# A fused two-layer transformer kernel: expert input rows split into bf16 halves before they are turned, and turned by a DMA transposition instead of TensorE

## The reference

```python
xf = x.reshape(-1, dim)                              # 8192 rows of 256
scores = softmax(xf @ w_router.T)
expert_weights, expert_indices = top_k(scores, 2)    # two of eight experts for each row
h = silu(einsum('td,edh->eth', xf, w1)) * einsum('td,edh->eth', xf, w3)   # hidden width 352
y = einsum('eth,ehd->etd', h, w2)
out = sum(expert_weights[:, :, None] * y[chosen experts], axis=1)
```

## Time and profile before

| | |
|---|---|
| times of three runs | 1982.25, 1982.32, 1988.02 us (median 1982.32) |
| span of the profiled execution, first to last instruction | 1987.6 us (it has no other time of its own; of the three runs, 1988.02 is the nearest) |
| first attention, up to about | 572 us |
| experts: count and tables, first load, then 71 tiles | 572 to 1050 us |
| second attention | 1050 to 1560 us |
| ternary feed-forward | 1560 to 1987 us |
| TensorE busy | 1746.9 us, 88% of the span |
| DVE, ACT, POOL busy | 1466.4, 1418.6, 1006.9 us |
| expert rounds | 6.3 to 6.4 us each |

### The profile page before, as it was taken

How to read it: one execution, slowest core, us unless ns; L and a number is a source line. 1 busy time by engine, 2 the same in 40 slices (tenths; PEclk the granted TensorE clock), 3 DMA queues, 4 the chain that set the end, 5 groups by cost and what they waited for, 6 DMA issues and landing times. The chain is left out here.

```text
span 1987.6 us, 52512 instructions
## 1 busy us (share of the span) xinstructions
PE 1746.9 (88%) x16125; PEld 1469.8 (74%) x16125; DVE 1466.4 (74%) x4269; ACT 1418.6 (71%) x2753; POOL 1006.9 (51%) x1295
## 2 busy tenths in 40 slices
PE   4889999999729999999993999999999578888887
PEld 3667878787519998999992788888888366666666
DVE  4889999999434343333332999999998599999996
ACT  5888999999424443444442777777777499999998
POOL 3557888887523233322226676676662133333332
PEclk8899999999859999999996999999999799999999
DMA  5434343433234352222224455545552112212111
GB/s 173 155 111 146 117 128 110 132 109 95 81 97 143 93 83 85 89 84 89 89 78 92 102 125 113 122 110 121 116 119 68 54 49 64 63 63 63 63 58 54
DMA packets 190557, 194.16 MB, mean 98 GB/s; under 512 B 33184, under 2 KB 180128, under 8 KB 189408
## 3 DMA queue, kind: packets, MB, share of 16 engines
q1 hardware_dynamic: 165856, 157.88, 26.7%
q0 software_dynamic: 24576, 34.62, 8.5%
HBM read 118.13 MB, written 74.30 MB: 97 GB/s over the span
## 5 line engine op out<-in xcount | busy, mean ns | idle before, releaser
L1898 POOL TENSOR_TENSOR e_h_lo<-e_h 128x256 bf16<-128x256 f32 (+1 forms) x213 | 138.7, 652 | 334.3 <-DVE e_h L2012 334.3
L2012 DVE TENSOR_TENSOR e_h<-e_s,e_ps_ab 128x256 f32<-128x256 f32 (+1 forms) x213 | 89.3, 420 | 275.2 <-ACT e_s L1921 275.2
L2073 PE MATMUL e_ps_ab<-e_xt_hi,k_w_hi 128*128 128x256 bf16 (+1 forms) x852 | 233.3, 274 | 0.0
L2073 PE MATMUL e_ps_ab<-e_xt_hi,k_w_lo 128*128 128x256 bf16 (+1 forms) x852 | 233.0, 273 | 0.0
L2073 PE MATMUL e_ps_ab<-e_xt_lo,k_w_hi 128*128 128x256 bf16 (+1 forms) x852 | 233.0, 273 | 0.0
L1921 ACT ACTIVATE e_s<-e_ps_ab 128x256 f32<-128x256 f32 (+1 forms) x213 | 81.5, 383 | 148.3 <-PE e_ps_ab L2073 148.2
L2473 PE MATMUL f_ps_h<-f_qh,p_arena 128*128 128x256 bf16 x512 | 123.8, 281 | 35.1 <-DVE f_ql L2437 28.5
L1928 ACT ACTIVATE e_yo<-e_ps_y,e_xe 128x256 f32<-128x256 f32 x142 | 59.6, 471 | 112.7 <-PE e_ps_y L2073 112.7
L2473 PE MATMUL f_ps_h<-f_ql,p_arena 128*128 128x256 bf16 x512 | 122.9, 279 | 0.0
L2073 PE MATMUL e_ps_y<-e_w_hi,e_h 128*128 (+1 forms) x426 | 116.5, 273 | 0.0
L2073 PE MATMUL e_ps_y<-e_w_hi,e_h_lo 128*128 (+1 forms) x426 | 115.9, 272 | 0.0
(11 more groups left out here) (433 smaller groups left out, 6621.5 us busy)
## 6 DMA issues: line engine op xcount, KB each, us to landing
e_xe<-sent_rows SPq DMA_DIRECT2D x71, 272.0 KB, 2.8
back_rows<-e_yo SPq DMA_DIRECT2D x71, 256.0 KB, 2.1
x_rows<-a_x SPq DMA_DIRECT2D x64, 256.0 KB, 2.7
p_arena<-in_xT SPq DMA_DIRECT2D x32, 256.0 KB, 4.7
a_xa<-in_x SPq DMA_DIRECT2D x32, 256.0 KB, 4.8
a_xr<-in_x SPq DMA_DIRECT2D x32, 256.0 KB, 4.6
a_xa<-x_rows SPq DMA_DIRECT2D x32, 256.0 KB, 3.3
x_rows<-a_xa SPq DMA_DIRECT2D x32, 256.0 KB, 2.2
```

What stands on the lines that cost most here:

```text
L1898: nc.gpsimd.tensor_tensor(h_lo[0:k, b.par, c, :], h[0:k, b.par, c, :], h_hi[0:k, b.par, c, :], ALU.subtract).then_inc(mg.sem, 1)
L2012: nc.vector.tensor_tensor(h[0:k, b.par, c, :], s[0:k, c, :], ps_ab[0:k, c, N:2 * N], ALU.mult).then_inc(mh.sem, 1)
L2073: last = nc.tensor.matmul(to, left, right, start=(i == 0), stop=(i == len(terms) - 1))
```

## The change

The rows of a tile are now split into halves as they lie, before they are turned: ACT reads `xe` in SBUF, in two activations of 128x256, and writes bf16 into a new buffer `rows` (two tiles deep); DVE subtracts in two instructions likewise. SP then issues one DMA transposition per tile (`turn`), from `rows` in SBUF to `turned` in SBUF: 128 partitions by 8 blocks of 128 bf16 numbers, 256 KB, three tiles deep. TensorE no longer turns anything and reads `turned`. The loads are six tiles deep instead of four. A new semaphore `t_ld` tells that a tile is turned; `up` waits for it, and so does `rows_high`, since the transposition of two tiles ago must have read `rows` before it is written again. The splitting runs further ahead: in round b, ACT and DVE split tile b+3 (before: b+1). SP stores b, turns b+3, loads b+6.

```diff
+    XE, XT = 6, 3
-        xe = sb("xe", [P, 4, NT, WIDE], F32)
-        xt_hi, xt_lo = sb("xt_hi", [P, 2, KC, N], BF16), sb("xt_lo", [P, 2, KC, N], BF16)
+        xe = sb("xe", [P, XE, NT, WIDE], F32)
+        rows_ = sb("rows", [P, 2, 2, KC, NT, P], BF16)
+        turned = sb("turned", [P, XT, 2, KC, N], BF16)
-        ps_t = psum("ps_t", [P, 2, 512])
+        t_ld = [sem(f"e_t_ld{i}") for i in range(XT)]
+        def turned_away(eng, b):
+            if b is not None:
+                eng.wait_ge(t_ld[b.n % XT], 16 * (b.n // XT + 1))
...
+            def turn(b):
+                uv.wait(sp, b, "lo")
+                me.wait(sp, b.back(XT), "up2")
+                nc.sync.dma_start_transpose(turned[:, b.n % XT, :, :, :].rearrange("p h k (t n) -> p (h k t) n", t=NT),
+                                            rows_[:, b.par, :, :, :, :].rearrange("p h k t n -> p (h k t n)")).then_inc(t_ld[b.n % XT], 16)
-            for b in tiles[0:4]:
+            for b in tiles[0:XE]:
                 load(b)
+            for b in tiles[0:XT]:
+                turn(b)
...
             for b in tiles:
                 store(b)
-                if b.n + 4 < TILES:
-                    load(tiles[b.n + 4])
+                if b.n + XT < TILES:
+                    turn(tiles[b.n + XT])
+                if b.n + XE < TILES:
+                    load(tiles[b.n + XE])
...
             def rows_high(b):
-                ue.wait(act, b, "xT")
-                me.wait(act, b.back(2), "up2")
-                nc.scalar.activation(xt_hi[:, b.par, :, :].rearrange("p k n -> p (k n)"), ps_t[:, b.par, :], ACT.Copy).then_inc(ua.sem, 1)
+                act.wait_ge(e_ld[b.n % XE], 16 * (b.n // XE + 1))
+                turned_away(act, b.back(2))
+                for t in range(NT):
+                    last = nc.scalar.activation(rows_[:, b.par, 0, :, t, :], xe[:, b.n % XE, t, 0:D].rearrange("p (k n) -> p k n", k=KC), ACT.Copy)
+                last.then_inc(ua.sem, 1)
...
                     silu(b, c, k)
-                    if c == 0 and 0 < b.n < TILES - 1:
-                        rows_high(tiles[b.n + 1])
+                    if c == 0 and b.n + 3 < TILES:
+                        rows_high(tiles[b.n + 3])
...
             def rows_low(b):
                 ua.wait(dve, b, "hi")
-                me.wait(dve, b.back(2), "up2")
-                nc.vector.tensor_tensor(xt_lo[:, b.par, :, :].rearrange("p k n -> p (k n)"), ps_t[:, b.par, :],
-                                        xt_hi[:, b.par, :, :].rearrange("p k n -> p (k n)"), ALU.subtract).then_inc(uv.sem, 1)
+                for t in range(NT):
+                    last = nc.vector.tensor_tensor(rows_[:, b.par, 1, :, t, :], xe[:, b.n % XE, t, 0:D].rearrange("p (k n) -> p k n", k=KC),
+                                                   rows_[:, b.par, 0, :, t, :], ALU.subtract)
+                last.then_inc(uv.sem, 1)
...
             def up(b, c, at, k, e):
-                ua.wait(pe, b, "hi")
-                uv.wait(pe, b, "lo")
+                turned_away(pe, b)
                 mh.wait(pe, b.back(1), f"h{c}")
...
                     up(b, c, at, k, e)
-                    if c == 0 and 0 < b.n < TILES - 1:
-                        turn_tile(tiles[b.n + 1])
```

More of the change, by code:

```diff
@@ L1772, in experts @@
         I32 = mybir.dt.int32
-        ident, bases, ends, tri, iota, starts, ones, seen = sh.ident, sh.bases, sh.ends, sh.tri, sh.iota, sh.starts, sh.ones, sh.seen
+        bases, ends, tri, iota, starts, ones, seen = sh.bases, sh.ends, sh.tri, sh.iota, sh.starts, sh.ones, sh.seen
         zeros, w1, w3 = sh.zeros, sh.w1, sh.w3
@@ L1823, in experts @@
         s_count = sem("e_count")
-        e_ld = [sem(f"e_e_ld{i}") for i in range(4)]
+        e_ld = [sem(f"e_e_ld{i}") for i in range(XE)]
+        t_ld = [sem(f"e_t_ld{i}") for i in range(XT)]
         o_st = [sem(f"e_o_st{i}") for i in range(2)]
@@ L1829, in experts @@
         uv = Signal(sem("e_uv"), "lo")
-        ue = Signal(sem("e_ue"), "xT")
         me = Signal(sem("e_me"), "up0 up1 up2")
@@ L1861, in load @@
                 at = sp.value_load(row[0:1, b.n:b.n + 1], min_val=0, max_val=E * ROOM + SPARE - ROWS)
-                if b.n >= 4:
-                    my.wait(sp, b.back(4), "y1")
-                sp.dma_start(xe[:, b.n % 4, :, :], block_of(at)).then_inc(e_ld[b.n % 4], 16)
+                if b.n >= XE:
+                    my.wait(sp, b.back(XE), "y1")
+                sp.dma_start(xe[:, b.n % XE, :, :], block_of(at)).then_inc(e_ld[b.n % XE], 16)
+            def turn(b):
[3 more added lines that the diff above has]
+                                            rows_[:, b.par, :, :, :, :].rearrange("p h k t n -> p (h k t n)")).then_inc(t_ld[b.n % XT], 16)
             def store(b):
@@ L1928, in results @@
                     nc.scalar.activation(yo[:, b.par, t, :], ps_y[:, b.par, t * D:(t + 1) * D], ACT.Copy,
-                                         scale=xe[:, b.n % 4, t, D:D + 1]).then_inc(my.sem, 1)
-            rows_high(tiles[0])
-            rows_high(tiles[1])
+                                         scale=xe[:, b.n % XE, t, D:D + 1]).then_inc(my.sem, 1)
+            for b in tiles[0:3]:
+                rows_high(b)
             for b in tiles:
@@ L2053, in prepare @@
                     nc.vector.tensor_scalar(pre.half_tg[:, :], pre.tg[:, 2:3], 0.5, None, ALU.mult).then_inc(wv, 1)
-            rows_low(tiles[0])
-            rows_low(tiles[1])
+            for b in tiles[0:3]:
+                rows_low(b)
             for b in tiles:
@@ L2059, in _ @@
                     hidden(b, c, k)
-                    if c == 0 and 0 < b.n < TILES - 1:
-                        rows_low(tiles[b.n + 1])
+                    if c == 0 and b.n + 3 < TILES:
+                        rows_low(tiles[b.n + 3])
                 if b.n == 4:
@@ L2074, in product @@
                 return last
[L2076 to L2081, removed]
             nc.tensor.matmul(ps_y[:, 1, 0:E], ones[:, :], seen[:, :], start=True, stop=True).then_inc(s_count, 1)
@@ L2099, in up @@
                     last = product(ps_ab[0:k, c, i * N:(i + 1) * N],
-                                   [(w[:, kc, bass.ds(e, 1), at:at + k].rearrange("p o k -> p (o k)"), x[:, b.par, kc, :])
-                                    for kc in range(KC) for w, x in ((hi, xt_hi), (hi, xt_lo), (lo, xt_hi))])
+                                   [(w[:, kc, bass.ds(e, 1), at:at + k].rearrange("p o k -> p (o k)"), turned[:, b.n % XT, part, kc, :])
+                                    for kc in range(KC) for w, part in ((hi, 0), (hi, 1), (lo, 0))])
                 last.then_inc(me.sem, 1)
@@ L2112, in down @@
                 last.then_inc(md.sem, 1)
-            turn_tile(tiles[0])
-            turn_tile(tiles[1])
             before = None
```

## The result

The changed kernel takes 1989.7 us (median of 20 runs, 1981.72 to 1997.95), the one before 1984.1 us on the same chip (20 runs, 1982.23 to 1988.3). The ratio is 1.0025, 95% interval 1.0016 to 1.0033: a quarter of a per cent slower, 5 to 6 us, where 2100 us was forecast, 117.5 us slower. Its profiled execution has a span of 1990.1 us, against 1987.6. So the direction was right by a hair and the size was wrong by a factor of twenty.

What follows compares the result with a forecast made beforehand. TensorE was taken to bound the expert stage before, the closed loop after, at 3.1 + 4.9 = 8.0 us a round: +112 us on 68 rounds, +5.5 for the start, so 1982.3 + 117.5 = 2100 us, range 1954 to 2350.

Steps and rivals of the forecast that it cites:

- a loop from `y1`: Expert stage: ACT's split waits for a transposition issued behind `y1`, closing one lap per round of 3.1 us plus transposition time.
- +112 us: Expert stage rounds: 8.0 us a round, 1.65 more than now, on 68 rounds.
- X: Time of one DMA transposition from issue to landing, taken as 4.9 us, ends 2.8 and 13.3 kept for the range.
- turning point: Transposition time of 3.25 us, issue to landing: under it the round gains, beyond it the round loses.
- no change: Balance case: transposition time in a narrow band from 3.1 to 3.3 us leaves the time unchanged; chance 0.06.
- 3.1 for the rest of the lap: Per round without the transposition: `y1` to store's issue 0.39, split 0.85, silu 0.76, `results` 0.84, hand-overs 0.24 us.
- the 30 us: TensorE in the expert stage: gain over 68 rounds from rounds of 5.9 us instead of 6.35.
- my rival of the copy's pace: Transposition lands in 2.8 us, the loop takes 5.9, just TensorE's round; time 1956 us, chance 0.22.
- 5 us for `places`: Queue of the early loads: once, the 13.3 us transfer `places` can delay a transposition, some 5 us left in the range.
- The removed transpositions: TensorE, between pieces 0 and 1 of a round: four transpositions cost 0.44 us.
- The longer start: Start of the expert stage: six loads instead of four go ahead of the first transposition; first product 5.5 us later.
- the rival in which the clock stays low: TensorE, busy 74%, falls to 1.2 GHz, its 54 products taking 11.5 us a round; time 2338 us, chance 0.10.

Runs made afterwards that it cites:

- experiment 1: Changed kernel with the transposition of tile b+3 issued ahead of the store of tile b: 1975.91 us, ratio 0.9894 to the kernel before.
- experiment 3: Changed kernel without the third product of each pair of halves, 42 matrix products a round instead of 54: ratio 0.9983 to the kernel before.
- experiment 4: Changed kernel with 42 matrix products a round instead of 54 and the transposition issued ahead of the store: 1894.6 us, ratio 0.9492 to the kernel before.
- experiment 9: Changed kernel with `rows` three tiles deep instead of two, loads still six deep, transposition behind the store: ratio 0.9919 to the kernel before.
- experiment 10: Changed kernel with each transposition issued as two, high halves and low halves, behind the store: ratio 1.0225 to the kernel before.
- experiment 11: Changed kernel with each transposition issued as two, high and low halves, ahead of the store: ratio 0.9868 to the kernel before.
- experiment 6: Changed kernel with `rows` three tiles deep instead of two and loads five deep instead of six: ratio 1.0569 to the kernel before.

## Why the prediction was wrong

**The mechanism was right.** The prediction put the bound in a loop from `y1` over the store's issue, the transposition, the split, silu and results, and experiments 1, 3, 4, 9, 10 and 11 all confirm it. That loop is why nothing was gained. The forecast of +112 us rested on two sizes in it. That the three turned tiles don't help, since the two-deep `rows` closes the loop, holds too: experiment 9 changes that depth alone and wins 1.0%.

**The step that failed is the size of X.** I took 4.9 us, scaling the price of a piece in `places` by 1024 pieces of 256 bytes. The trace after shows that there are 1024 such packets per tile, but each takes 18 ns at the median, some 21 on average in a quiet round, and the whole lands in 3.2 us; the price of a 16-byte piece written to memory does not carry over to these 256-byte pieces written to SBUF. The other row, `slot_i`, had given 2.9, and the nearest plain row, the load of 272 KB, 2.8. The sum's largest term, +112 us, hung on that choice, between two rows that disagreed by 2 us a round around a turning point at 3.25. I saw the turning point and still gave no change 0.06; it is what came, with a median X inside the band of 3.1 to 3.3.

**A second term was mis-sized, 3.1 for the rest of the lap.** It measures 2.5 to 2.6. I had added durations; activations in a row overlap, so two splits take 0.72 and not 0.85, two silus 0.63 and not 0.76, and the hand-overs are largely in that. With X = 3.2 and 2.6, the quiet lap is 5.8 and the gain would have been the 30 us less the start, as in my rival of the copy's pace. My 3.1 with the right median X gives a round of 6.3, so no change: right by luck, since the 0.5 us too much stands where the spread of X should.

**Why that gain did not come.** The mean of X up to the start of the split is 3.84 us, not its median of 3.26, and 2.6 + 3.84 = 6.44, against a measured mean round of 6.42. A loop 0.15 us under TensorE's 5.90 can absorb next to nothing of a long X, so the average is what counts. That X varies was left out, but for 5 us for `places`, which cost 10.2 us over two rounds here and 3.4 before. Why X varies is open in part: the packets of instructions coincide with the long ones, and no run took them away.

**The smaller terms.** The removed transpositions are worth 0.44 us a round: right, rounds of 5.90 where nothing else binds. The longer start: 5.5 us forecast; first load to first product went from 5.6 to 10.2 us, so 4.6. The splits on ACT and DVE are 0.41 and 0.42 us a piece, and hidden, apart from the lap. The clock stayed at 1.00 but for the 10.2 us behind `places`. There 26 products went at 0.21 us apart instead of 0.11 (752.45 to 757.96), so the fall cost some 2.6 us of the 10.2, an estimate; the rival in which the clock stays low is not what happened. (Its sum has a slip: 54 products at 0.21 are 11.3 us, not 11.5, and its time 2328.)

The Trainium skill's rule that transposing DMAs are as fast as ordinary ones (Advanced Engine Details and Errata, X-Bar Transpose (TRN2)) is near the trace: 3.2 us against 2.4 for the store of the same size, and 1.3 us of issue against 0.36. By the Trainium skill's 1309 ns for a block of 128x128 (VectorE: DVE Perf Modes, The three transpose paths), an estimate: eight blocks in a row would be 10.5 us; the trace has all eight in 3.2.

## What to carry to other kernels

When a change adds a wait, follow what stands behind the waiting instruction until the chain meets itself: a lap that closes within one round is a bound of its own, whatever the depth of the buffers off it, and it is cut by moving one issue ahead of one wait. Size such a lap by pitches and not by durations, and by the mean of its DMA time and not the median; where it comes out within 0.2 us of the other bound, as here, expect the long transfers to eat the gain. And an experiment that buys room for one buffer with another changes two things.

## What the runs showed of the hardware

A transposition by DMA from SBUF to SBUF, 128 partitions by 8 blocks of 128 bf16 numbers (256 KB), takes SP 1.26 to 1.32 us to issue, where it isn't held up, and lands 3.2 us (median) after the start of its issue; half of it takes 1.26 and 2.5 (experiment 10). It moves as 1024 packets of 256 bytes, 18 ns each at the median.

A packet of 16384 bytes of instructions took 0.9 to 1.35 us in 36 of 38 cases in the changed kernel. Transpositions that overlapped one had an X of 4.2 us on average, 4.5 in those over 3.4, and the others 3.3. There was one such packet for every 95 to 97 matrix products, so every 11.3 us in the changed kernel (rounds of 6.42 us) and every 14.1 us in experiment 6 (7.95 us).

64 KB written from SBUF to memory in 4096 pieces of 16 bytes took 11.3 to 13.6 us to land; in 128 pieces of 512 bytes, 2.8.

At the 11.2 us transposition in the changed kernel TensorE was idle from 745.1 to 752.45. The granted clock fell to 0.5 at 747.7 and came back at 758.0; in between the products started 0.21 us apart instead of 0.11.
